# Moving 32 indirect scatters of a counting sort from two later stages to the expert stage, and issuing them there without pacing

## The reference

```python
# layer 0, last part: eight experts, each node goes to one of them (capacity 489 rows)
x = x + _L0_ffn_ref(_layernorm(x, axis=-1)[None], L0_ffn_gate_w, ..., L0_ffn_w1, L0_ffn_b1, L0_ffn_w2, L0_ffn_b2)[0]
# layer 1, first part: graph convolution over 53,125 edges beside a linear attention (needs the Gram matrix of xn)
xn = _layernorm(x, axis=-1)
x = x + _L1_gnn_ref(xn, edge_attr_4, edge_attr_10, ..., src, dst) + _L1_mix_ref(xn[None], ...)[0]
# layer 1, last part: a gate that is itself a graph attention over 32,768 other edges, then four experts
x = x + _L1_ffn_ref(_layernorm(x, axis=-1)[None], L1_ffn_edge_index, ...)[0]
```

## Time and profile before

| what | value |
|---|---|
| median of 3 runs | 2801.38 us (2801.19 to 2802.84) |
| the profiled execution's own time | 2804.37 us |
| its span in the trace | 2802.7 us |
| mean granted clock of PE | 0.865 |
| busy: PE, PEld, DVE, ACT, POOL | 2206.6, 1477.4, 1928.9, 1409.5, 1585.7 us |
| all 256 scatters (L2076) | 251.9 us busy, first at 1103.8 us, last at 1557.4 us |

### The profile page before, as it was taken

How to read it: one execution, slowest core, us unless ns; L and a number is a source line. 1 busy time by engine, 2 the same in 40 slices (tenths; PEclk the granted TensorE clock), 3 DMA queues, 4 the chain that set the end, 5 groups by cost and what they waited for, 6 DMA issues and landing times. The chain is left out here.

```text
span 2802.7 us, 41395 instructions
## 1 busy us (share of the span) xinstructions
PE 2206.6 (79%) x11128; PEld 1477.4 (53%) x11128; DVE 1928.9 (69%) x4009; ACT 1409.5 (50%) x4483; POOL 1585.7 (57%) x1695
## 2 busy tenths in 40 slices
PE   6996777777777756869996687877878699999774
PEld 3544555555555545746652433333335687788763
DVE  4565999999999888811117899999997433323787
ACT  2221655566655634511126599999996322222242
POOL 2645666666666212667677777777775177777000
PEclk9998888888888875579996899999999589999998
DMA  3214667666667110313323333333331311111005
GB/s 110 59 46 129 203 200 211 201 198 194 207 202 203 36 62 21 104 50 109 110 66 101 108 104 105 104 104 103 104 105 38 89 31 39 39 39 34 14 1 196
DMA packets 167619, 292.87 MB, mean 104 GB/s; under 512 B 53832, under 2 KB 101965, under 8 KB 167398
## 3 DMA queue, kind: packets, MB, share of 16 engines
q0 software_dynamic: 77520, 186.78, 24.0%
q1 hardware_dynamic: 80720, 87.10, 9.9%
q10 hardware_dynamic: 9158, 16.33, 1.6%
HBM read 253.35 MB, written 36.75 MB: 104 GB/s over the span
## 5 line engine op out<-in xcount | busy, mean ns | idle before, releaser
L2499 PE MATMUL cv_ps<-cv_msg,cv_hot 128*128 128x512 f32 x880 | 421.4, 615 | 116.1 <-DVE acc L2561 84.4
L2486 POOL DMA_INDIRECT cv_x<-x_tab,e_src x440 | 425.8, 968 | 139.8 <-issue 92.6
L2517 ACT ACTIVATE cv_msg<-cv_x,factors 128x64 f32<-128x64 f32 x1320 | 357.8, 336 | 0.0
L2912 POOL DMA_INDIRECT gs_h<-h_tab,fc_q x280 | 264.4, 944 | 155.4 <-issue 82.8
L657 POOL DMA_INDIRECT at_kv_tail<-kv_tab,e_src x272 | 264.7, 973 | 149.5 <-PE at_a L1136 76.2
L2499 PEld LDWEIGHTS cv_ps<-cv_msg,cv_hot 128*128 128x128 f32 x880 | 159.6, 194 | 342.1 <-ACT cv_msg L2517 170.8
L2076 POOL DMA_INDIRECT pairs<-gating_pair,gating_place x256 | 251.9, 984 | 125.5 <-issue 62.2
L2561 DVE TENSOR_TENSOR acc<-acc,cv_ps 128x256 f32 x880 | 308.9, 416 | 8.9 <-PE cv_ps L2499 5.5
L1111 PE MATMUL at_q<-q_parts,at_hot_n 128*128 x1320 | 228.4, 329 | 41.4 <-DVE at_kv_head L1208 17.2
L2514 ACT ACTIVATE cv_msg<-cv_x,factors 128x256 f32<-128x256 f32 x440 | 218.4, 496 | 18.0 <-DMA cv_x<-x_tab,e_src 17.9
L2866 ACT ACTIVATE gs_x_hid<-gs_x_h,x_b 128x128 f32<-128x128 f32 x320 | 91.2, 368 | 270.5 <-PE gs_x_h L2833 270.5
(11 more groups left out here) (571 smaller groups left out, 4710.8 us busy)
## 6 DMA issues: line engine op xcount, KB each, us to landing
x_space<-in_L_ffn_w SPq DMA_DIRECT2D x16, 1024.0 KB
at_rel_row<-e_rel_rows SPq DMA_DIRECT2D x55, 256.0 KB, 4.2
experts_out<-gs_y ACTq DMA_DIRECT2D x20, 512.0 KB
x_y<-experts_out SPq DMA_DIRECT2D x20, 512.0 KB, 8.0
cv_x<-x_tab,e_src POOLq DMA_INDIRECT x440, 2.7
kv_tab<-p_qkv SPq DMA_DIRECT2D x25, 256.0 KB, 2.0
gs_h<-h_tab,fc_q POOLq DMA_INDIRECT x280, 2.3
at_kv_tail<-kv_tab,e_src POOLq DMA_INDIRECT x272, 3.8
```

Of the source, the lines that this page charges most:

```text
L2486: nc.gpsimd.indirect_dma_start(out=xg[:, i % RT, u, :], out_offset=None, in_=x_tab, in_offset=bass.IndirectOffsetOnAxis(ap=e.src[:, t:t + ...
L2499: nc.tensor.matmul(ps[u % R][:, :], hot[:, i % 2, u, :], msg[:, i % 2, u, :], start=True, stop=True).then_inc(summed, 1)
L2517: ins = nc.scalar.activation(parts[:, 1, 1 + m], xg[:, i % RT, u, 0:M], ACT.Copy, scale=factor[:, t:t + 1, 1 + m])
L2912: nc.gpsimd.indirect_dma_start(out=hg[:, i % RT, u, :], out_offset=None, in_=h_tab, in_offset=bass.IndirectOffsetOnAxis(ap=e.src[:, i * U ...
```

## The change

All turns from 6 to 31 are now issued in `experts0`, 208 scatters in place of 176, and `pace` is gone: a scatter there waits only for the turn two before its own. `return0` and `gram1` issue none. The rest of the kernel is the same.

```diff
-            def pace(n):
-                per = scatter.turns * U // NE
-                e, x = n // per, n % per * 16 // per
-                marks = []
-                if 0 < x <= 8 or e and not x:
-                    marks.append((h_done, e * FC + x))
-                elif x > 8:
-                    marks.append((y_done, e * len(TC) + (x - 8) // 2))
-                return [(sem, count) for sem, count in marks if count > 0]
-
             @block.gpsimd
             def _(pool):
-                scatter.run(nc, k, pool, pairs, pair, place_i, pace=pace)
+                scatter.run(nc, k, pool, pairs, pair, place_i)
...
@@ return0
-        scatter = Scatter(s, "re_sc_", RETURN_SCATTER, GRAM_SCATTER)
...
-                scatter.run(nc, k, pool, pairs, pair, place_i)
                 ef.angles(pool, angular)
...
 SORT_SCATTER = 6
-RETURN_SCATTER = C2 // U - 4
-GRAM_SCATTER = RETURN_SCATTER + 2
+RETURN_SCATTER = C2 // U
...
@@ Scatter.run
-    def run(self, nc, k, pool, pairs, pair, place_i, pace=None):
+    def run(self, nc, k, pool, pairs, pair, place_i):
...
-                if pace is not None:
-                    for sem, count in pace(i * U + u):
-                        pool.wait_ge(sem, count)
                 self.one(nc, pairs, pair, place_i, i, c)
...
@@ gram1
-        scatter = Scatter(s, "g1_sc_", GRAM_SCATTER, C2 // U)
...
-                scatter.run(nc, k, pool, pairs, pair, place_i)
```

More of the change, by code:

```diff
@@ L1589, in _, with return0 @@
                 turn(NE // 2 - 1, last=True)
-def return0(nc, k, out_buf, slot_i, factor, ef, angular, stats, pairs, pair, place_i, x0):
+def return0(nc, k, out_buf, slot_i, factor, ef, angular, stats, x0):
     with Scope(nc) as s:
@@ L2197, in angles, with gram1 @@
         pool.wait_ge(self.turned_in, 16 * G1)
-def gram1(nc, k, a, x_tab, sums, e, ef, angular, factor, pairs, pair, place_i):
+def gram1(nc, k, a, x_tab, sums, e, ef, angular, factor):
     with Scope(nc) as s:
@@ L3423, in program @@
                     stats = LayerStats(nc, t, k, "n2_")
-                    return0(nc, k, slots_out, slot_i, factor, ef, angular, stats, pairs2, pair, place_i, x0)
+                    return0(nc, k, slots_out, slot_i, factor, ef, angular, stats, x0)
                 recycle_semaphores(nc)
@@ L3433, in program @@
                         sums = t2.sb("sums", [P, 3, D + 1])
-                        gram1(nc, k, a, x_tab, sums, e1, ef, angular, factors, pairs2, pair, place_i)
+                        gram1(nc, k, a, x_tab, sums, e1, ef, angular, factors)
                         convolve(nc, k, e1, x_tab, factors, sums, acc, (angular, pair, place_i))
```

## The result

| | before | after |
|---|---|---|
| median (7 runs each) | 2803.22 us | 2813.44 us |
| lowest to highest | 2801.19 to 2807.85 | 2812.28 to 2816.92 |
| span of the profiled execution | 2802.7 us | 2811.2 us |

The ratio is 1.0037, with a 95% interval of 1.0026 to 1.0049: the changed kernel is slower, by 10.2 us between the medians and by 7 to 14 us within the interval. The prediction was 2815.2 us, within 2812 to 2819, so the measured 2813.44 us lies inside.

What follows compares the result with a forecast made beforehand. PE was taken to set the expert and Gram stages' length, with every border waiting for POOL's scatters. Expert +20.5, return -6.7 and Gram 0 gave +13.8 us on 2801.38, so 2815.2 us, range 2812 to 2819.

Steps and rivals of the forecast that it cites:

- The border reading: At stage borders: no engine passes until POOL's scatters have landed, so POOL's stream is part of every stage's length.
- Expert stage, predicted +20.5: Expert stage: 208 scatters at 1.263 us end POOL's issue 21.0 us later, shifting the border by 20.2 to 21.0 us.
- the long unpaced run shows no gap but 0.305 us, and I take the same for the rest: Expert stage: the 63 scatters from 1375.9 to 1454.2 us gave the rate of 1.263 us assumed for all 208.
- Pacing, predicted to give 19.4 of the 40.4 us back: Expert stage: 32 more scatters cost POOL 40.4 us, of which the removed pacing waits give 19.4 back.
- Return stage, predicted -6.7: Return stage: without scatters POOL finishes early, DVE ends the stage, and it is 6.7 us shorter (6.4 to 6.9).
- the 0.8 us that the prediction allowed: Return stage: a rise of PE's clock at its start would shorten it by at most 0.8 us; taken as 0.
- The bound of 1 us for a faster DVE: Return stage: DVE's gain from no scatters running beside it was put at 0, with 1 us as the bound.
- Gram stage, predicted 0: Gram stage: its 16 scatters are hidden behind PE, so no change; 0.3 us gain or 2 us loss allowed.
- A return stage that pays in full: Rival, return stage: it shortens by all of POOL's 26.6 us, giving -6.1 us, 2795.3 us; chance 0.03.
- The Gram stage kept its clock: Rival, Gram stage: PE's clock stays low, up to +25 us more, 2840 us; chance 0.05.
- The scatters held their rate: Rival, expert stage: unpaced scatters do not hold 1.263 us, another 64 us at 1.58 each, 2879 us; chance 0.02.
- The signs of being wrong: L1643 starting before 1477 or after 1480, DVE's groups changing length, or over 10 us gained behind the expert stage.

Runs made afterwards that it cites:

- unpaced_only: The kernel before with only the pacing removed, its 176, 16 and 16 scatters left in place: 2801.12 us against 2803.77, ratio 0.9992.
- return_only: The kernel before, unpaced, with only the return stage's scatters moved beside the experts (192 there, 16 in Gram): 2793.89 us, ratio 0.9970.
- gram_only: The kernel before, unpaced, with only the Gram stage's scatters moved beside the experts (192 there, 16 in return): 2806.20 us, ratio 1.0007.
- spread: The kernel before, unpaced, scatters divided 40 in the sort, 192 experts, 8 return, 16 Gram: 2787.68 us against 2802.45, ratio 0.9946.
- all_paced: The changed kernel's split, all 208 scatters beside the experts, with the pacing waits of the kernel before kept: 2829.33 us, ratio 1.0086.
- before_again: The kernel before, unchanged, profiled once more: 2798.91 us, one run.
- after_again: The changed kernel, with nothing further changed, profiled once more: 2814.96 us, one run.

## Why the prediction was right

**The border reading held.** "A border lets no engine pass until POOL's scatters have landed" is borne out from both sides. Where POOL was last, the border came 1.64 to 1.66 us after the end of its issue in six profiles, for 192 and for 208 scatters, paced and unpaced. Where POOL was 18 us early (unpaced_only) the border did not follow it. What no run separates is the landing from the issue: the last scatter of return_only, gram_only and spread landed 2.1 us after its start, some 0.5 us ahead of the border, and its landing follows its issue by the same time in each. That POOL waits for the landing there stands in the kernel's text, at the end of `Scatter.run`.

**Expert stage, predicted +20.5, measured +21.4 and +21.1.** Both lie above the prediction's own bounds for this term, 20.2 to 21.0. Two errors of size partly cancel. The last issue ends 264.11 us after the stage's start, where the sum gave 262.8: POOL's rate was 1.263 us as read, but once, at 1356.59, the gap was 1.70 us instead of 0.30. The step that was off in size is "the long unpaced run shows no gap but 0.305 us, and I take the same for the rest": the run that I read began after that place. And the border follows POOL by 1.65 us, not by "some 2.0".

**Pacing, predicted to give 19.4 of the 40.4 us back.** unpaced_only confirms 18.0 (241.82 - 223.79; 19.4 less the 1.4 of the pause). all_paced shows that this is no fixed price of the waits: with 26 scatters to an expert the same pacing costs 10.6 us.

**Return stage, predicted -6.7, measured -7.5 and -7.7.** DVE became the end, as forecast. Its last instruction now ends 64.6 us after the stage's start instead of 65.1: the 0.5 us wait for ACT is gone, and the clock of PE rose earlier. Nothing ties this to the change. The kernel before does the same in its second profile: in before_again DVE's last instruction ends at 64.65 us, without that wait, after a rise some 20 us into the stage, while return_only, without scatters in this stage, has the late rise (33 us) and the wait, and a return stage of 66.65 us. So 0.5 of the 7.5 us goes with the clock and is luck, as far as these runs show. The windows of PE alone (busy, granted clock, DMA share, GB/s) show it, answering to the earlier trace rows:

```profile
1490.00:1497.00 7.00, 7.00 (x30) 0.50 0.54 164
1497.00:1500.00 3.00, 3.00 (x24) 0.89 0.42 125
```

And before_again, whose return stage starts at 1457.35:

```profile
1457.40:1475.00 17.60, 16.84 (x56) 0.50 0.42 121
1475.00:1480.00 5.00, 5.00 (x32) 0.79 0.49 150
```

In the changed kernel the rise comes between 1497 and 1500, some 20 us after the stage's start, where it took 37 in the first profile of the kernel before. The stage still began with 19 us at 0.50 (1.2 GHz), in which PE was busy for all but 0.6 us. The nine profiles have the rise between 19 and 38 us into the stage, and what sets it stays open. The gain from the earlier rise is inside the 0.8 us that the prediction allowed. The Trainium skill, "TensorE: Matmul & The Clock Gate", Part 1, says that a busy TensorE soon gets its full clock; this stage does not show that in either kernel. The rest of the miss is the border, 1.54 us after DVE instead of 1.77. The bound of 1 us for a faster DVE was not needed, nor had the scatters blocked DVE: DVE was busy for 54.08 us against 54.12.

**Gram stage, predicted 0, measured -0.04.** gram_only shows the same by itself, -0.0 us with 16.8 us less work of POOL.

**The whole.** The three stages give +13.9 and +13.4 us in two pairs of profiles, beside a forecast of +13.8. That the first agrees to 0.1 us is luck: the expert stage came out 0.9 us above its term and the return stage 0.8 below. The medians of seven runs give only 10.2, with an interval that ends at 13.7, and the time of 2813.44 us lies in the range by the help of a kernel before that measured 1.84 us slower than the median the sum was added to.

The profiles show where the difference lies. The profiled executions themselves differ by +8.5 us in the first pair (spans of 2802.7 and 2811.2) and by +16.1 in the second (2797.2 and 2813.3). Outside the three stages, the time ahead of the expert stage, where no instruction was changed, differs by -1.3 and +2.9 us, and the gate stage, from the clearing of `score` to DVE's next stage, by -5.8 and -0.1; between the Gram and the gate stage it is +0.4 in both. The kernel before differs by 4.0 us with itself in that gate stage. So the missing 3 us need no cause in the change, and what the shift does to later stages is not shown beyond the +0.4.

**The rivals.** A return stage that pays in full would be 47 us long; it is 66. (For that, DVE's five groups of 9.6 us would have had to shrink by some 20 us, two fifths and not a quarter; a little over a quarter goes with the break-even of 20.5 us.) The Gram stage kept its clock (0.92 in both windows). The scatters held their rate but for the one pause. The signs of being wrong did not appear either: DVE's first `slot_i` started at 1477.84, between 1477 and 1480, DVE's work kept its length, and the return and Gram stages gained 7.5 us together, not over 10.

## What to carry to other kernels

Where stages end in a barrier of all engines, background work on an idle engine is free only up to the time of the slowest other engine, and each item beyond it costs its full issue time, here 1.26 us (changed kernel against return_only). Count for each stage how many items its cover holds, and place them by that, not by where the engine looks least busy on average. Here the Gram stage hid its 16 scatters and the return stage 8 of 16. The experts took 192 for about a microsecond and 208 for 21. The sort hid neither 48 nor 40, but with 40 POOL ends 2.9 us after DVE instead of 9.6. Moving all out of the later stages cost 10 us (7 to 14), and dividing them by cover won 15 (8 to 22).

## What the runs showed that I had not expected

In all five unpaced kernels (in after_again too), and in all_paced, POOL makes one pause of 1.70 us in place of 0.30, always about 144 us after the expert stage's first scatter where it is unpaced: before the 162nd scatter in after, unpaced_only, return_only, gram_only and all_paced, and before the 154th in spread, which has eight fewer in the sort. That is the 114th of the expert stage each time. At the same place the kernel before waits for PE, 4.85 us, and from there to the stage's end it has no gap beyond the usual one. Slow landings do not explain it: in the changed kernel the scatters of the 9 us before it had landed in 2.1 us each. What it is stays open.

A scatter of the expert stage takes up to 7.5 us to land instead of 2.1 (the tile's row in the changed kernel gives 2.1 at least and in the middle, 7.5 at most). Those between 1340 and 1347, while rows and weights of an expert were loading (DMA share 0.92), took 5.7 to 6.0. It still delays nothing, since only the turn after next waits for it, some 10 us later.
